# A wait half-way in each chunk's gathers, for ScalarE's copies of the chunk in the other buffer

## The chip, the cores and the metric

The kernel runs on one core of a Trainium2 chip. The metric is the device time of one execution in microseconds. "Profiled execution" means the one that the hardware profiler recorded; "span" is the time from its first to its last recorded instruction.

## The reference, cut to what matters

Two graph networks follow each other over the same 6250 nodes and 200000 edges, sorted by destination. The change touches the second, a transformer over the edges with three layers:

```
src, dst = edge_index[0], edge_index[1]
edge_attr = _mlp(_ln(edge_embed, eng, enb), eW1, eb1, eW2, eb2)
for l in range(L):                                    # L = 3, H = 8 heads, D = 64
    h = _ln(x, n1g[l], n1b[l])
    xi, xj = (h[dst], h[src])
    q = (xi @ Wq[l] + bq[l]).reshape(-1, H, HD)
    kn = (xj @ Wkn[l] + bkn[l]).reshape(-1, H, HD)
    ke = (edge_attr @ Wke[l] + bke[l]).reshape(-1, H, HD)
    vn = (xj @ Wvn[l] + bvn[l]).reshape(-1, H, HD)
    ve = (edge_attr @ Wve[l] + bve[l]).reshape(-1, H, HD)
    alpha = (q * (kn + ke)).sum(-1) / scale
    ...                                               # softmax over the edges of one destination
    msg = ((vn + ve) * alpha[..., None]).reshape(-1, D)
    agg = jax.ops.segment_sum(msg, dst, num_segments=n)
    ...                                               # gate, output product, MLP on the nodes
```

## The kernel before

Edges lie in the order of their destination, 1568 on each of 128 partitions (`T`), and are handled in `NCH` = 28 chunks of `C` = 56 edges a partition. Each layer (`Fori(0, L)`) first makes a table `tabkv` in HBM, one row of 128 floats per node, key and value projection side by side. Then comes the edge loop, `Fori(0, NCH // 2)` with two chunks a turn, `u` = 0 and 1 being the buffer; on ScalarE the last two chunks stand behind the loop. After it, `fix_and_fetch` joins the partitions' ends, and the node part follows. Before all this there is a first part (the first network and the edge MLP), which has gathers of its own from another table.

In the edge loop the engines do this for chunk c, counted over the layers as n:

- GpSimd (line 561 on): waits for the indices `srcI` of the buffer and for `done1`, which VectorE raises at the end of a chunk; it starts at 2 and GpSimd waits for n + 1, so chunk n - 2, the last user of the buffer, must be done. Then `gathers` sends 56 indirect DMAs (line 505), each of which fetches one row of `tabkv` for each of the 128 partitions into `G1[:, u, t, :]`. The semaphore is `got1[u][t // 8]`: eight gathers make one of the seven (`PT`) blocks.
- TensorE (lines 700 to 717): for each step s = 0 to 6 it waits for block s and for free PSUM, and makes keys and values of 8 edges a partition: it copies G1 by the identity (line 712) and adds the edge features' product (line 715). Three pairs of PSUM banks go round, so TensorE may be up to three steps ahead of ScalarE's copies (`v_moved`); the last matmul of a step raises `kv_ready`. With its last step it raises `seen1`, which lets SyncE load new indices.
- VectorE: spreads the queries by eight scans (line 1298), then multiplies the keys of each step by the queries (line 1305, waits for `kv_ready`, raises `k_used`), sums the products (line 1308), scans for the maxima, multiplies the values by the weights (line 1321, reads the value half of G1) and scans them in nine rows (line 1328). Then it raises `done1`.
- ScalarE: after each `k_used` it copies the step's values from PSUM back into the value half of G1 (line 909) and raises `v_moved`. It starts at 3, and seven copies a chunk are made, so 7 n + 3 means that all values of the chunks before n are copied. Then it lays out the next chunk's queries (line 901), makes the exponentials (lines 913 to 915), and stores the chunk's rows (lines 918, 920).
- SyncE loads indices, queries (line 467) and edge features (line 469) for the chunks ahead.

`hold` is a wait followed by one increment of a bookkeeping semaphore that nobody waits for in this loop.

Of the kernel before, what the change touches and what calls it, by code (L numbers as in the profile page):

```python
# [13 lines left out]
C = 56  # L14
NCH = 28
# [12 lines left out]
PT = C // 8  # L28
# [27 lines left out]
def build(nc, A, out):  # L56
# [5 lines left out]
    def dram(name, shape, dt=f32):  # L62
        return nc.dram_tensor(name, shape, dt, kind="Internal").ap()

    tab0 = dram("tab0", (NT * P, W0))
    tabkv = dram("tabkv", (NP, 2 * D))
# [18 lines left out]
    with ctx:  # L85
# [3 lines left out]
        def sem(name):  # L89
            return ctx.enter_context(nc.semaphore(name))  # L90
# [52 lines left out]
        waits_sp, waits_pool, waits_pe = sem("waits_sp"), sem("waits_pool"), sem("waits_pe")  # L143
# [30 lines left out]
        got1 = [[sem(f"got1_{u}_{k}") for k in range(PT)] for u in range(2)]  # L174
# [4 lines left out]
        v_moved = sem("v_moved")  # L179
# [101 lines left out]
        G1 = sb("G1", [P, 2, C, 2 * D])  # L281
# [29 lines left out]
        def hold(eng, passed, s, value):  # L311

            eng.wait_ge(s, value)
            eng.sem_inc(passed, 1)
# [176 lines left out]
        def _(pool):  # L491
# [8 lines left out]
                                      [[1, w], [0, C]], base=0, channel_multiplier=0, **exact)  # L500
            last.then_inc(pool_c, 1)

            def gathers(u, G, tab, got):
                for t in range(C):
                    nc.gpsimd.indirect_dma_start(out=G[:, u, t, :], out_offset=None, in_=tab[:, :],  # L505
                                                 in_offset=IND(ap=srcI[:, u, t:t + 1], axis=0)).then_inc(got(t), 16)


            pool.wait_ge(n0_tab, 16 * NG)
            pool.wait_ge(idx0[0], 16)  # L510
            gathers(0, G0, tab0, lambda t: got0[0])

            pool.wait_ge(p_rp, 16)
# [9 lines left out]
            pool.wait_ge(p_dve, 6)  # L523
            pool.wait_ge(idx0[1], 16)
            gathers(1, G0, tab0, lambda t: got0[1])
            with pool.Fori(1, NCH // 2) as i:
                for u in range(2):
                    pool.wait_ge(idx0[u], 16 * i + 16)
                    hold(pool, waits_pool, done0, 2 * i + u + 1)
                    gathers(u, G0, tab0, lambda t: got0[u])  # L530

            def fix_and_fetch(st, R, o, outs, rows):

                for out_, stored in outs:
                    hold(pool, waits_pool, out_, stored)
                nc.gpsimd.indirect_dma_start(out=rfix[:, 0:R], out_offset=None, in_=st[:, :],
                                             in_offset=IND(ap=fixI[:, 0:1], axis=0)).then_inc(f_got, 16)
                hold(pool, waits_pool, f_dve, o * 5 + 5)
                nc.gpsimd.indirect_dma_start(out=st[:, :], out_offset=IND(ap=fixI[:, 0:1], axis=0),
                                             in_=wfix[:, 0:R], in_offset=None).then_inc(f_put, 16)  # L540
                hold(pool, waits_pool, f_put, o * 16 + 16)
                for j in range(NT):
                    nc.gpsimd.indirect_dma_start(out=rows[:, j, :], out_offset=None, in_=st[:, :],
                                                 in_offset=IND(ap=endI[:, j:j + 1], axis=0)).then_inc(rows_got[j // 8], 16)
# [4 lines left out]
            with pool.Fori(0, L) as l:  # L549

                for j in range(NT):
                    if j % 8 == 0:
                        hold(pool, waits_pool, a_dve, l * A_DVE + 2 * NB + j // 8 + 1)
                    nc.gpsimd.indirect_dma_start(out=qexp[:, :], out_offset=IND(ap=startI[:, j:j + 1], axis=0),
                                                 in_=q_all[:, j, :], in_offset=None).then_inc(q_put, 16)
                hold(pool, waits_pool, q_dram, l * 16 + 16)
                nc.gpsimd.indirect_dma_start(out=qb[:, :], out_offset=None, in_=tabq[:, :],
                                             in_offset=IND(ap=firstI[:, 0:1], axis=0)).then_inc(q_first, 16)
                for k in range(2):
                    hold(pool, waits_pool, a_out[k], (l + 1) * (16 * ((NB + 1 - k) // 2)))  # L560
                hold(pool, waits_pool, h_out, (l + 1) * 32)
                with pool.Fori(0, NCH // 2) as i:
                    for u in range(2):
                        c = 2 * i + u
                        pool.wait_ge(idx1[u], l * (NCH // 2 * 16) + i * 16 + 16)
                        hold(pool, waits_pool, done1, l * NCH + c + 1)
                        gathers(u, G1, tabkv, lambda t: got1[u][t // 8])
                fix_and_fetch(st1, R1, l + 1, [(st1_out, (l + 1) * (16 * NCH) + 16)], rows1)


# [869 lines left out]
```

## Time and profile before

| what | us |
|---|---|
| median of 3 runs | 12879.86 |
| lowest and highest run | 12839.82, 12920.56 |
| profiled execution, its time | 12850.77 |
| its span | 12849.0 |
| GpSimd busy | 7420.7 (58%) |
| VectorE busy | 5378.1 (42%) |
| TensorE matmuls busy | 5153.0 (40%) |
| ScalarE busy | 2820.9 (22%) |

In a row of the timeline the first number is the start in us from the span's start, the second the time it took (of a merged row: the busy time of its xcount instructions), and the brackets hold how long the engine was idle before it and what ended this wait. "issue" there means that the engine waited for nothing the profile shows, and "remote" another core or an unknown queue (this kernel has one core). In the page's group lines, busy time and mean of one stand first behind the bar, then the idle time just before these instructions. TensorE's matmuls are pipelined and their ends are modelled.

### The profile page before, as it was taken

Reading aid. Unit: us, or ns where it says so; the run is one execution under the profiler, and the core shown is the slowest. Engines: PE = TensorE matmul, PEld = TensorE weight load, DVE = VectorE, ACT = ScalarE, POOL = GpSimd, SP = SyncE. Lnnn points to the kernel's source line nnn. Section 1 sums busy time; section 2 is a strip of 40 time slices with the busy share of each in tenths; the row PEclk is TensorE's granted clock in tenths of the full one; section 3 lists DMA queues with packets and bytes.
Section 4 is the critical chain, followed back from the end, with each engine's and each line's share of the span. In section 5 each row is a group of like instructions: output and inputs, shape, how many; then the busy total and the mean of one; then the engine's idle time right before and its main releaser. Section 6 shows DMA issues by size and latency. Waiting matters only on the chain.

```text
span 12849.0 us, 55197 instructions
## 1 busy us (share of the span) xinstructions
PE 5153.0 (40%) x13727; PEld 2796.8 (22%) x13727; DVE 5378.1 (42%) x8026; ACT 2820.9 (22%) x2709; POOL 7420.7 (58%) x6688
## 2 busy tenths in 40 slices
PE   9455554444433333333343333333324233333334
PEld 6322222222211121122211111212112121121122
DVE  3355555544432433444332344344342333433444
ACT  0022222222211211222121122122122112212222
POOL 2488888888745555556525555555544455555552
PEclk9977777777766666666666666666667666666667
DMA  1233333333332322333213223323222222322331
GB/s 33 49 121 120 121 118 111 121 123 111 114 111 77 106 98 97 100 103 119 92 38 104 94 97 106 98 97 110 95 89 73 90 96 94 115 92 95 108 97 46
DMA packets 402907, 1246.37 MB, mean 97 GB/s; under 512 B 194869, under 2 KB 251766, under 8 KB 357926
## 3 DMA queue, kind: packets, MB, share of 16 engines
q0 software_dynamic: 213664, 428.57, 12.7%
q1 hardware_dynamic: 169030, 468.05, 10.3%
q10 hardware_dynamic: 20160, 349.23, 6.9%
q14 instruction: 43, 0.35, 0.0%
q8 instruction: 10, 0.16, 0.0%
HBM read 807.54 MB, written 437.84 MB: 97 GB/s over the span
## 4 chain that ended last, share of the span: by engine, by line
another core or an unknown queue 25%; DVE 22%; issue 19%; POOL 17%; PE 10%; DVEq 3%; ACT 2%; DMA 1%; SPq 0%; ACTq 0%; POOLq 0%
POOL G L505 16%; DVE SX L1328 5%; DVE QQ L1298 5%; DVE SX L1321 4%; PE PS L590 3%; PE PS L712 2%; DVE al L1308 2%; DVE PX L1305 2%; PE PS L715 2%; DVEq L1329 1%; DVEq L1299 1%; DVE SX L1314 1%; PE PS L736 1%; ACT QQ L901 1%
## 5 line engine op out<-in xcount | busy, mean ns | idle before, releaser
L505 POOL DMA_INDIRECT G<-tabkv,srcI x4704 | 4438.4, 944 | 3568.3 <-DVEq L1329 2127.9
L712 PE MATMUL PS<-G,ident 128*128 128x512 f32 x2352 | 1617.4, 826 | 5128.3 <-ACT G L909 3497.1
L505 POOL DMA_INDIRECT G<-tab,srcI x1568 | 2579.8, 1645 | 731.0 <-issue 501.6
L1305 DVE TENSOR_TENSOR PX<-PS,QQ 128x512 f32<-128x512 f32 x588 | 610.2, 1060 | 4647.5 <-remote 3557.6
L712 PEld LDWEIGHTS PS<-G,ident 128*128 128x128 f32 x2352 | 558.8, 252 | 5767.2 <-ACT G L909 3624.3
L715 PE MATMUL PS<-Wkvp,EA 128*128 128x256 f32 x4704 | 1329.9, 422 | 386.0 <-issue 384.9
L909 ACT ACTIVATE G<-PS 128x512 f32<-128x512 f32 x588 | 351.0, 597 | 5133.1 <-issue 3332.1
L644 PE MATMUL PS<-hid,W2p 128*128 128x512 f32 x1568 | 774.4, 640 | 1419.5 <-ACT hid L827 960.4
L715 PEld LDWEIGHTS PS<-Wkvp,EA 128*128 128x128 f32 x4704 | 1050.9, 223 | 930.3 <-issue 803.1
L918 ACT ACTIVATE S<-SX 128x4480 f32<-128x4480 f32 x84 | 688.2, 8193 | 1279.9 <-DVEq L1329 1264.6
L1328 DVE TENSOR_TENSOR_SCAN SX<-PS,SX 128x456 f32<-128x456 f32 x756 | 763.2, 1082 | 12.2
L1298 DVE TENSOR_TENSOR_SCAN QQ<-PS,QQ 128x456 f32<-128x456 f32 x672 | 679.5, 1083 | 209.4 <-issue 145.8
L637 PE MATMUL PS<-xT,W1p 128*128 128x512 f32 x1568 | 715.4, 599 | 76.0 <-ACT xT L806 56.8
L644 PEld LDWEIGHTS PS<-hid,W2p 128*128 128x128 f32 x1568 | 307.3, 206 | 1768.0 <-ACT hid L827 1031.7
L1094 DVE TENSOR_TENSOR al<-G,ewC 128x56 f32<-128x56 f32 x28 | 6.9, 247 | 1415.2 <-DMA G<-tab,srcI 1415.2
L901 ACT ACTIVATE QQ<-QQ 128x3584 f32<-128x3584 f32 x84 | 539.3, 6421 | 264.6 <-DMA QQ<-qexp 264.6
L1321 DVE TENSOR_TENSOR SX<-G,PS 128x3584 f32<-128x3584 f32 x84 | 526.6, 6269 | 87.8 <-ACT PS L914 80.5
L827 ACT ACTIVATE hid<-PS,b1c 128x512 f32<-128x512 f32 x784 | 488.5, 684 | 264.5 <-PE PS L637 254.9
L1124 DVE TENSOR_TENSOR_SCAN S<-ee,S,G 128x56 f32<-128x56 f32 x1792 | 412.8, 317 | 2.1
L1118 DVE TENSOR_TENSOR_SCAN S<-maskC,S,G 128x56 f32<-128x56 f32 x1792 | 411.3, 316 | 0.0
L637 PEld LDWEIGHTS PS<-xT,W1p 128*128 128x128 f32 x1568 | 295.4, 191 | 458.1 <-issue 387.0
L590 PE MATMUL PS<-S 128*49 128x128 bf16 x1568 | 372.2, 416 | 3.4 <-DVE S L1007 3.4
(287 smaller groups left out, 4450.0 us busy)
## 6 DMA issues: line engine op xcount, KB each, us to landing
st<-S ACTq DMA_DIRECT2D x84, 2240.0 KB
QQ<-qexp SPq DMA_DIRECT2D x84, 1792.0 KB
EA<-eaT SPq DMA_DIRECT2D x84, 1792.0 KB
st<-S ACTq DMA_DIRECT2D x28, 3668.0 KB
G<-tabkv,srcI POOLq DMA_INDIRECT x4704
xe<-in_edge_attr SPq DMA_DIRECT2D x28, 1792.0 KB
qexp<-zeros SPq DMA_DIRECT2D x28, 1792.0 KB
eaT<-eaC ACTq DMA_DIRECT2D x28, 1792.0 KB
```

Source lines behind the costliest of these rows:

```text
L505: nc.gpsimd.indirect_dma_start(out=G[:, u, t, :], out_offset=None, in_=tab[:, :], in_offset=IND(ap=srcI[:, u, t:t + 1], axis=0)).then_inc( ...
L590: last = mm(PS[0:NT, 7, 0:P], oh[u][:, t, 0:NT], oh[u][:, t, NT:OHW], start=False, stop=False, skip_group_check=True)
L637: last = mm(PS[:, 1 + 2 * r + kh, :], W1p[:, r, kh, :], xT8[:, :], start=True, stop=True)
L644: last = mm(PS[:, 5, :], W2p[:, kh, r, :], hid8[:, r, kh, :], start=(r == 0 and kh == 0), stop=(r == 1 and kh == 1))
L712: mm(PS[:, b + k, :], ident[:, :], G1[:, u, 8 * s + 4 * k:8 * s + 4 * k + 4, :], start=True, stop=False, skip_group_check=True)
L715: last = mm(PS[:, b + j // 2, 2 * P * (j % 2):2 * P * (j % 2) + 2 * P], EA[:, u, 4 * s + j, :], Wkvp[:, :], start=False, stop=True, skip_g ...
L901: f(Qf[:, :, 1:CX], Q1.rearrange("p c d -> p d c"), ACT.Copy).then_inc(q_flat, 1)
L918: f(S1[:, :, :], SX[:, :, 1:CX].rearrange("p r c -> p c r"), ACT.Copy).then_inc(s_rows, 1)
L1298: scan(rows, gate8f, rows, 0.0, ALU.mult, ALU.add)
L1305: tt(PR[:, 8 * s:8 * s + 8, :], kv_of(b)[:, :, 0:D], Qf[:, :, 1 + 8 * s:9 + 8 * s].rearrange("p d t -> p t d"), ALU.mult).then_inc(k_used, 1)
L1321: tt(SX[:, 2 * H:R1, 1:CX].rearrange("p (j h) x -> p j h x", h=H), G1[:, u, :, D:2 * D].rearrange("p t (h d) -> p d h t", h=H), score8[:, ...
L1328: scan(rows, gate8f, rows, 0.0, ALU.mult, ALU.add)
```

## The change

`gathers` gets a parameter for which of the 56 gathers it sends, all by default. In the edge loop GpSimd sends the first 28, waits until `v_moved` is at 7 n + 3, and sends the other 28.

```
-            def gathers(u, G, tab, got):
-                for t in range(C):
+            def gathers(u, G, tab, got, steps=range(C)):
+                for t in steps:
                     nc.gpsimd.indirect_dma_start(out=G[:, u, t, :], out_offset=None, in_=tab[:, :],
                                                  in_offset=IND(ap=srcI[:, u, t:t + 1], axis=0)).then_inc(got(t), 16)
...
                         pool.wait_ge(idx1[u], l * (NCH // 2 * 16) + i * 16 + 16)
                         hold(pool, waits_pool, done1, l * NCH + c + 1)
-                        gathers(u, G1, tabkv, lambda t: got1[u][t // 8])
+                        gathers(u, G1, tabkv, lambda t: got1[u][t // 8], range(C // 2))
+                        hold(pool, waits_pool, v_moved, (l * NCH + c) * PT + 3)
+                        gathers(u, G1, tabkv, lambda t: got1[u][t // 8], range(C // 2, C))
```

## Rows read from the trace of the kernel before

**Rows 1.** The page: span, then two groups; busy, mean | idle before, its releaser.
```profile
span 12849.0 us, 55197 instructions
L505 POOL DMA_INDIRECT G<-tabkv,srcI x4704 | 4438.4, 944 | 3568.3 <-DVEq L1329 2127.9
L1305 DVE TENSOR_TENSOR PX<-PS,QQ 128x512 f32<-128x512 f32 x588 | 610.2, 1060 | 4647.5 <-remote 3557.6
```

**Rows 2.** The view of line 1305: what ended its idle time (us, times).
```profile
  remote: 3557.6, 174
```

**Rows 3.** The timeline of VectorE over one chunk's steps.
```profile
8104.84 3.00 DVE L1305 TENSOR_TENSOR PX<-PS,QQ 128x512 f32<-128x512 f32 x3
8112.71 1.08 DVE L1305 TENSOR_TENSOR PX<-PS,QQ 128x512 f32<-128x512 f32 x1 [4.88 <-issue]
8129.98 1.05 DVE L1305 TENSOR_TENSOR PX<-PS,QQ 128x512 f32<-128x512 f32 x1 [16.20 <-remote]
8162.18 1.06 DVE L1305 TENSOR_TENSOR PX<-PS,QQ 128x512 f32<-128x512 f32 x1 [31.15 <-remote]
8173.43 1.06 DVE L1305 TENSOR_TENSOR PX<-PS,QQ 128x512 f32<-128x512 f32 x1 [10.19 <-remote]
...
8189.88 9.09 DVE L1328 TENSOR_TENSOR_SCAN SX<-PS,SX 128x456 f32<-128x456 f32 x9
...
8208.89 2.02 DVE L1305 TENSOR_TENSOR PX<-PS,QQ 128x512 f32<-128x512 f32 x2
```

**Rows 4.** The timeline of TensorE in the same chunk, its steps 3, 4 and 6.
```profile
8106.57 3.78 PE L712 MATMUL PS<-G,ident 128*128 128x512 f32 x4 [23.20 <-ACT G L909]
...
8112.51 1.88 PE L712 MATMUL PS<-G,ident 128*128 128x512 f32 x4
...
8119.40 1.88 PE L712 MATMUL PS<-G,ident 128*128 128x512 f32 x4
```

**Rows 5.** The timeline of GpSimd: first and last of these 56 gathers, the next chunk's first.
```profile
8095.30 0.94 POOL L505 DMA_INDIRECT G<-tabkv,srcI  x1 [13.82 <-DVEq L1329]
...
8163.96 0.94 POOL L505 DMA_INDIRECT G<-tabkv,srcI  x1 [0.30 <-issue]
8199.80 0.94 POOL L505 DMA_INDIRECT G<-tabkv,srcI  x1 [34.90 <-DVEq L1329]
```

**Rows 6.** The timeline where two chunks' gathers follow without a gap: GpSimd, then VectorE.
```profile
4877.43 0.94 POOL L505 DMA_INDIRECT G<-tabkv,srcI  x1 [20.85 <-DVEq L1329]
...
5015.98 0.94 POOL L505 DMA_INDIRECT G<-tabkv,srcI  x1 [0.30 <-issue]
...
4983.94 1.05 DVE L1305 TENSOR_TENSOR PX<-PS,QQ 128x512 f32<-128x512 f32 x1 [29.87 <-remote]
5017.54 1.06 DVE L1305 TENSOR_TENSOR PX<-PS,QQ 128x512 f32<-128x512 f32 x1 [32.55 <-remote]
5032.96 3.01 DVE L1305 TENSOR_TENSOR PX<-PS,QQ 128x512 f32<-128x512 f32 x3 [14.36 <-remote]
```

**Rows 7.** The timeline at a layer's start: first gathers of chunks 0 and 1; VectorE.
```profile
3813.45 0.96 POOL L505 DMA_INDIRECT G<-tabkv,srcI  x1 [10.22 <-DMA srcI<-in_src]
...
3883.36 0.94 POOL L505 DMA_INDIRECT G<-tabkv,srcI  x1 [0.30 <-issue]
...
3911.23 1.06 DVE L1305 TENSOR_TENSOR PX<-PS,QQ 128x512 f32<-128x512 f32 x1 [31.84 <-remote]
...
3969.33 2.03 DVE L1305 TENSOR_TENSOR PX<-PS,QQ 128x512 f32<-128x512 f32 x2 [22.75 <-remote]
```

**Rows 8.** Stretches: a layer's first gather of chunk 1 to its last product; length, then busy.
```profile
3883.40:6522.10 2638.70, 898.58 (x2289) 519.63 (x2287) 1073.60 (x975) 544.81 (x327) 1426.71 (x1512) 0.65 0.30 98
6910.40:9553.90 2643.50, 904.46 (x2282) 520.97 (x2281) 1073.29 (x975) 544.87 (x327) 1426.56 (x1512) 0.64 0.30 97
9941.40:12569.40 2628.00, 898.04 (x2285) 519.75 (x2284) 1073.71 (x975) 544.89 (x327) 1426.54 (x1512) 0.64 0.30 98
```

**Rows 9.** The timeline of ScalarE: the last copy of values of the chunk in rows 3.
```profile
8174.52 0.60 ACT L909 ACTIVATE G<-PS 128x512 f32<-128x512 f32 x1 [10.65 <-DVE PX L1305]
```

## Prediction

> **What bounds the kernel now.** I read the page first. The span is 12849.0 us, and the largest groups belong to the layer loops: 4704 gathers on GpSimd, and 588 products of line 1305 on VectorE, before which VectorE sat idle for 4647.5 us, 55 us in each of the 84 chunks [rows 1]. So VectorE is not the bound by its work, and GpSimd is not either, since it too waits for VectorE (`DVEq L1329`) for 2127.9 us [rows 1]. Something keeps both waiting. The view of line 1305 says what ended VectorE's waits: for 3557.6 us "remote", which means that no instruction in the trace explains it [rows 2].
>
> So I followed one chunk in the timeline. VectorE takes steps 0 to 2 together at 8104.84, because TensorE was three ahead, and step 3 at 8112.71. Step 4 it starts at 8129.98, step 5 at 8162.18, step 6 at 8173.43 [rows 3]. The only semaphore it waits for is `kv_ready`, which the last matmul of the step raises. But TensorE's matmuls of steps 3 to 6 begin at 8106.57, the first step taking 5.9 us and each other 3.44 ((8119.40 - 8112.51) / 2), so by the trace step 5 ends at 8119.4 and step 6 at 8122.8 [rows 4]. The signals of steps 5 and 6 therefore reach VectorE 40 to 50 us after the modelled ends of the matmuls. The reader is to see when they come: one per 32 us while GpSimd sends gathers, and then the rest at once.
>
> When is "then"? The gathers of this stretch begin at 8095.30, and the last is issued at 8163.96, so they follow each other by 68.66 / 55 = 1.25 us [rows 5]. The last step starts 78.1 us after the first gather. Elsewhere two chunks' gathers run without a gap, from 4877.43 to 5015.98, 112 of them at the same pace (138.55 / 111 = 1.25). There VectorE gets a step at 4983.94 and one at 5017.54, 33.6 us apart, and then three in 3.01 us at 5032.96, 155.5 us after the first gather [rows 6]. At the start of a layer it is the same: two chunks in a row from 3813.45, a step at 3911.23, and the last two together at 3969.33, 155.9 us after the first [rows 7]. So 56 gathers hold the signals back for 78.1 us and 112 for 155.5 to 155.9 us: 1.39 us a gather, more than the 1.25 us at which they are issued. My reading: something serves 1.39 us for each gather, and while it is behind, a step of TensorE gets through only every 32 to 34 us; when it has caught up, all finished steps get through. I call that moment F. The mechanism itself I can't see in the trace; the rule I read off three places, of two lengths of burst.
>
> The chain of a chunk is then: gathers of chunk n hold back the steps of chunk n-1, VectorE ends chunk n-1 25.5 us after its last step (8173.43 to the end of the nine scans, 8189.88 + 9.09) [rows 3], that raises `done1`, and only then may the gathers of chunk n+1 start. From the first gather of chunk 1 to the last product, the three layer loops take 2638.7, 2643.5 and 2628.0 us [rows 8], 7910.2 in sum; per chunk about 97.
>
> **The change part by part.** It removes nothing and adds one wait per chunk on GpSimd, behind the 28th gather, for the copies of all values of the chunk before (`v_moved`), with one increment of a bookkeeping semaphore. The instruction itself costs well under a microsecond, which I take from how fast GpSimd goes on after such a wait: VectorE's scans end at 8198.97 and the next gather starts at 8199.80 [rows 3, 5]. I take 0.8 us. Queued behind it are 28 gathers of 1.25 us, 35 us of issue, and behind these the gathers of the next chunk; who waits for them is TensorE in steps 3 to 6 of chunk n.
>
> What it does to time follows from F. (a) The first 28 gathers are served after 28 x 1.39 = 38.9 us instead of 77.8, if nothing was pending. (b) At F the remaining steps reach VectorE: three products in 3.0 us [rows 6], ScalarE's last copy starts 1.1 us after the last product starts and takes 0.6 [rows 3, 9], and GpSimd goes on 0.8 us later. So the second half starts at F + 1.95 + 1.1 + 0.6 + 0.8 = F + 4.4. I call this moment R. (c) VectorE goes on from its last product as before and takes the first product of the next chunk 35.5 us later (8173.43 to 8208.89) [rows 3], at R + 33. (d) GpSimd has issued the second half at R + 35. The next chunk's first half needs `done1` of chunk n-1, raised at R - 2.5 + 25.5 = R + 23, so it follows without a gap. GpSimd's waits for `DVEq L1329` go, and those 56 gathers, second half and next first half, are one burst served until R + 56 x 1.39 = R + 77.8. (e) In this burst TensorE must bring the next chunk's seven steps. Steps 0 to 2 it does at once after R, when their blocks have landed (24 gathers of the first half) and nothing is held back yet: in the chunk shown, step 3 still came through 17 us after the burst began [rows 3]. They are ready at R + 33. Step 3 begins at R + 36 and gets through after some 33.5 us, at R + 70. Steps 4 and 5 have run and wait for F. Step 6 needs the copy of step 3, at R + 71.5, and up to 5.9 us on TensorE (the slow first step, 8106.57 to 8112.51) [rows 4], so it ends about at F. (f) At F = R + 77.8 three products, the copy, and the next R is F + 4.4.
>
> The period is then 77.8 + 4.4 = 82.2 us when step 6 is done by F, and about 84 when it misses F by 2 us; I take 83, for 97 before. The wait costs GpSimd 83 - 70 = 13 us a chunk, and this is no loss, since it waited longer for `done1` before.
>
> **The sum**, for one layer loop, from the first gather of chunk 1. To the first R: the burst is then 56 + 28 = 84 gathers from 69.9 us before it [rows 7], so F is at 116.8 - 69.9 = 46.9, and R at 51. Then 26 periods of 83 = 2158. Then from the last R to the last product: products 0 to 2 at 33 to 35, and four steps at TensorE's own pace, because only 28 gathers are in flight, served at 38.9: 5.9 + 3 x 3.44 = 16.2, so 52 in all. Together 2261, for 2638.7, 2643.5 and 2628.0 before. Three layers: 6783 for 7910.2, a gain of 1127. The first part of the kernel doesn't run this code: `gathers` is only given a parameter there, with the old default. The profiled execution took 12850.77 us, 1.8 us over its span, and the median of the runs is 12879.86, 0.2% above it. 12850.77 - 1127 = 11724.
>
> **Bounds of what the trace doesn't show.** It has no break inside a chunk's gathers. How fast the held-back signals come after 28 gathers I bound by nothing faster than the issue itself (35 us) and nothing slower than the share of the long bursts (38.9 us); I take the latter, since three bursts of two lengths fit it. For how soon after R steps are held back again, the bounds are 17 us and more (the step that got through in rows 3) and, at the worst, at once; I take the 17, which is enough to have steps 0 to 2 through. The worse end is the first rival. Nothing bounds the loss at zero: if the signals don't come in the break, GpSimd stands still and its gathers come later.
>
> **The rivals.** *The break is too short.* The signals of steps 1 and 2 are not out before the service is behind again. Then step 1 comes at about R + 67, and steps 2 and 3 only at F. Step 5 needs the copy of step 2 and step 6 that of step 3, so TensorE runs both after F: 1.8 + 5.9 + 3.4 = F + 11.1, R is 2.5 us behind that, and the period is about 91. 51 + 26 x 91 + 52 = 2469 a layer, 7407 for the three, 503 less than before: about 12350. For it: in the chunk of rows 3 only step 3 comes through in the burst before the 32 us rhythm begins, and the break is only 4 us. Against it: at 5032.96 three steps come in 3 us, so what is pending goes at once.
>
> *The signals don't depend on the gathers* (slower). They come late by a clock of their own, 57 to 78 us after the chunk began, whatever GpSimd does. Then the wait ends 60 to 80 us after the first gather, on average 73; 35 us of gathers follow, and the period is 73 + 35 = 108 for 97: 81 x 11 = 890 more, 13740. The point from which it decides: the change loses when the wait ends later than 97 - 35 = 62 us after the chunk's first gather. Against it: 155.5 us for 112 gathers and 78.1 for 56 are the same 1.39 each; a clock of its own would not scale. By the Trainium skill, "SBUF — State Buffer", section "Who interferes with whom", this would be the case: a DMA never contends with a compute engine, and PE waits on no one. The trace does not agree as far as it goes: the steps' signals stop and go with the gathers, by 40 to 50 us; what the two share it does not tell.
>
> *Nothing changes.* The copies are all done when the wait is reached, 35 us after the chunk's first gather. In the chunk shown the last copy starts at 8174.52, 79 us after it [rows 9], so this can be so in few chunks: 12850.
>
> *Nothing is held back at all*, because no burst is long: GpSimd then issues without pause, 70 us a chunk, 11724 - 26 x 3 x 13 = about 10700. Against it: the service, not the issue, would then be behind again, as in the bursts of 112.
>
> **How the numbers follow.** The forecast (period 82 to 86, 11650 to 11960) gets 0.6, the too short break 0.22, the signals on their own clock 0.1, no change 0.04, nothing held back 0.04. The predicted time is that of the first, 11724. The range must reach to the second, 12350, and a period 1.3 us longer (26 x 3 x 1.3 = 100): 12450. At the other end, a service that has caught up a microsecond sooner, as the scatter of the bursts allows, gives a period of about 81, 2 us under the 83, 26 x 3 x 2 = 156: 11570, and I begin at 11550. Left out is 0.1 + 0.04 + 0.04. Faster by over 1%: 0.6 + 0.22 + 0.04 = 0.86; within 1%: 0.04; slower by over 1%: 0.1. About 1% is what a measurement of this kernel can tell from no change, its three runs lying 0.6% apart.
>
> **What would show it.** In the profile after: GpSimd's waits for `DVEq L1329` nearly gone in the layer loops, and in their place one of some 13 us per chunk before the 29th gather, ended by ScalarE's copies (L909), about 1000 us in all. VectorE with three products in 3 us just ahead of that gather's start. VectorE's idle time before line 1305 down from 55 to about 41 us a chunk. Gathers still 944 ns, 1.25 us apart. The forecast is wrong if the 29th gather starts much later than 45 us after a layer's burst of 28, or if VectorE still gets single steps 32 us apart behind the break.

## The result, and the profile after

| what | us |
|---|---|
| changed kernel, median of 4 runs | 11651.4 (11649.46 to 11656.92) |
| kernel before, beside it, median of 4 | 12859.84 (12741.78 to 12920.56) |
| ratio | 0.9058, 95% interval 0.9014 to 0.9102 |
| forecast | 11724, range 11550 to 12450 |

The change makes the kernel 9.4% faster. One sentence belongs to this number from the start, though nothing in the profile before hinted at it: in two of the later jobs the kernel before itself took 10547 and 10560 us, and in the one of them in which the changed kernel ran too, the change is worth nothing (run `after_b` below).

The page of the changed kernel first, the same groups as in [rows 1]; all lines behind 566 have moved by 2 (1305 is 1307 now, 909 is 911, 1328 is 1330; in the kernels of the experiments the lines move by some others, and the names of the tiles stay):

```profile
span 11655.1 us, 55365 instructions
L505 POOL DMA_INDIRECT G<-tabkv,srcI x4704 | 4438.9, 944 | 2460.5 <-issue 1408.0
L1307 DVE TENSOR_TENSOR PX<-PS,QQ 128x512 f32<-128x512 f32 x588 | 602.5, 1058 | 3430.5 <-remote 3216.5
```

A gather still takes 944 ns. GpSimd's idle time before gathers fell from 3568.3 to 2460.5 us, VectorE's before its products from 4647.5 to 3430.5, 55.3 to 40.8 us a chunk. VectorE's end of a chunk no longer stands among what GpSimd waits for. The view of GpSimd's waits (us in total, times, longest) has ScalarE's copies in its place:

```profile
POOL G L505 <- issue: 1909.5, 6187, 2.2
POOL G L505 <- ACT G L911: 1021.9, 81, 17.3
```

The timeline of GpSimd around two waits, and of VectorE between them:

```profile
7128.09 0.94 POOL L505 DMA_INDIRECT G<-tabkv,srcI  x1 [0.30 <-issue]
7141.09 0.94 POOL L505 DMA_INDIRECT G<-tabkv,srcI  x1 [12.06 <-ACT G L911]
...
7209.74 0.94 POOL L505 DMA_INDIRECT G<-tabkv,srcI  x1 [0.30 <-issue]
7223.17 0.94 POOL L505 DMA_INDIRECT G<-tabkv,srcI  x1 [12.48 <-ACT G L911]
...
7155.21 9.09 DVE L1330 TENSOR_TENSOR_SCAN SX<-PS,SX 128x456 f32<-128x456 f32 x9
...
7174.99 2.99 DVE L1307 TENSOR_TENSOR PX<-PS,QQ 128x512 f32<-128x512 f32 x3
7185.31 1.07 DVE L1307 TENSOR_TENSOR PX<-PS,QQ 128x512 f32<-128x512 f32 x1 [7.33 <-remote]
7216.11 1.05 DVE L1307 TENSOR_TENSOR PX<-PS,QQ 128x512 f32<-128x512 f32 x1 [29.73 <-remote]
7219.70 2.06 DVE L1307 TENSOR_TENSOR PX<-PS,QQ 128x512 f32<-128x512 f32 x2 [2.53 <-remote]
```

The second half starts at 7141.09 (this is the R of the prediction), and 56 gathers run without a gap until 7209.74. The last two steps come together at 7219.70, 78.6 us after R. The next R is 3.5 us later, at 7223.17: 82.1 us for this chunk. The layer loops, first gather of chunk 1 to last product as in [rows 8]:

```profile
3891.00:6128.00 2237.00, 799.82 (x2291) 480.38 (x2289) 1079.14 (x976) 545.94 (x327) 1426.80 (x1512) 0.67 0.34 115
6515.20:8750.00 2234.80, 793.11 (x2288) 476.37 (x2289) 1078.88 (x975) 546.24 (x328) 1426.77 (x1512) 0.68 0.34 115
9139.90:11376.70 2236.80, 795.93 (x2286) 478.74 (x2284) 1078.21 (x975) 545.93 (x327) 1426.82 (x1512) 0.67 0.35 115
```

The second stretch ends 1.3 us too early, for that layer's last product starts at 8751.25. So it is about 6710 us for 7910, 1200 less, and the profiled execution took 1193.9 less than before (11656.92 for 12850.77). All of the gain is in the layer loops. The busy time of VectorE, ScalarE and GpSimd has hardly changed there; that of TensorE's matmuls, as the trace models them, went from 2701 to 2389 us, but TensorE waits for most of a loop in both kernels. It is waiting that went.

One thing more stands in this trace, and it was in that of the kernel before too: not only the signals are late. Towards the end of the step that TensorE makes last before its long wait, its own matmuls come one by one. Its timeline in the same chunk:

```profile
7194.39 0.38 PE L717 MATMUL PS<-Wkvp,EA 128*128 128x256 f32 x1 [2.29 <-issue]
7197.19 0.40 PE L717 MATMUL PS<-Wkvp,EA 128*128 128x256 f32 x1 [2.42 <-issue]
```

They are 2.80 us apart, with one weight load between them, so 1.40 us an instruction. Inside a step, two matmuls of this line start 2.8 us apart in 82 places of this trace and in 34 of the kernel before's, where 2.1 us, in 54, is more frequent; in the later runs in which nothing is held back (`after_b`, `e_sw`) they are never more than 0.4 us apart.

### The profile page after: what moved, and what is told of

Read it like the earlier page. It is cut to its first block, busy times and chain, and to the rows that moved or that the text cites. A ratio compares the mean times of both kernels' runs of the same rounds, so it can differ in the third digit from the quotient of the medians.

```text
span 11655.1 us, 55365 instructions
## 1 busy us (share of the span) xinstructions
PE 4839.1 (42%) x13727; PEld 2670.5 (23%) x13727; DVE 5393.2 (46%) x8026; ACT 2825.5 (24%) x2709; POOL 7427.5 (64%) x6688
## 3 DMA queue, kind: packets, MB, share of 16 engines
q1 hardware_dynamic: 169030, 468.05, 11.1%
## 4 chain that ended last, share of the span: by engine, by line
another core or an unknown queue 30%; DVE 27%; issue 18%; PE 10%; DVEq 5%; POOL 5%; ACT 3%; DMA 2%; SPq 0%; ACTq 0%; POOLq 0%
DVE SX L1330 6%; DVE QQ L1300 5%; DVE SX L1323 4%; POOL G L505 3%; PE PS L592 3%; DVE PX L1307 2%; PE PS L646 2%; DVE al L1310 2%; PE PS L639 2%; DVE S L1126 2%; DVE S L1120 2%; DVEq L1309 1%; ACT QQ L903 1%; DVEq L1331 1%
## 5 line engine op out<-in xcount | busy, mean ns | idle before, releaser
L505 POOL DMA_INDIRECT G<-tabkv,srcI x4704 | 4438.9, 944 | 2460.5 <-issue 1408.0
L714 PE MATMUL PS<-G,ident 128*128 128x512 f32 x2352 | 1435.0, 742 | 4252.3 <-ACT G L911 3390.1
L1307 DVE TENSOR_TENSOR PX<-PS,QQ 128x512 f32<-128x512 f32 x588 | 602.5, 1058 | 3430.5 <-remote 3216.5
L714 PEld LDWEIGHTS PS<-G,ident 128*128 128x128 f32 x2352 | 519.7, 230 | 4839.8 <-ACT G L911 3559.6
L717 PE MATMUL PS<-Wkvp,EA 128*128 128x256 f32 x4704 | 1207.5, 395 | 377.4 <-issue 377.3
L717 PEld LDWEIGHTS PS<-Wkvp,EA 128*128 128x128 f32 x4704 | 963.0, 205 | 783.6 <-issue 680.6
L554 POOL DMA_INDIRECT qexp<-PX,startI x147 | 140.9, 958 | 369.9 <-DVEq L1288 326.0
```

Of the source, the lines that this page charges most:

```text
L714: mm(PS[:, b + k, :], ident[:, :], G1[:, u, 8 * s + 4 * k:8 * s + 4 * k + 4, :], start=True, stop=False, skip_group_check=True)
L717: last = mm(PS[:, b + j // 2, 2 * P * (j % 2):2 * P * (j % 2) + 2 * P], EA[:, u, 4 * s + j, :], Wkvp[:, :], start=False, stop=True, skip_g ...
L1307: tt(PR[:, 8 * s:8 * s + 8, :], kv_of(b)[:, :, 0:D], Qf[:, :, 1 + 8 * s:9 + 8 * s].rearrange("p d t -> p t d"), ALU.mult).then_inc(k_used, 1)
```

## The experiments

Theory 1 is that of the prediction: gathers in flight hold back TensorE's step signals, with 1.39 us of service for each; when it has caught up, at F, all pending steps come. Jobs are independent, and each has its own runs of the kernel before; ratios are only taken inside a job.

**The first job: where the wait stands, what it waits for, and how much TensorE does.** The kernel before took 12851.24 us in it (median of 7).

`e_kv` waits for TensorE's last signal instead of ScalarE's last copy:

```
-                        hold(pool, waits_pool, v_moved, (l * NCH + c) * PT + 3)
+                        hold(pool, waits_pool, kv_ready, (l * NCH + c) * PT + 1)
```
(`kv_ready` starts at 1 in it, and VectorE's wait for it is one higher.)

> The changed kernel, but GpSimd's wait behind the 28th gather is for the last step's signal from TensorE (kv_ready) instead of ScalarE's last copy (v_moved). Theory 1 (the gathers in flight hold back TensorE's step signals; when their service has caught up, at a moment F, all pending ones go, and GpSimd may go on): the changed kernel goes on 3.4 us after F (two products 1.95 us apart with 1.1 + 0.6 for the copy and 0.8 for GpSimd); here it goes on 0.8 us after F, so the period falls from 82.0 to about 79.6 us, 78 periods x 2.4 = 190 us, 11460 us. Rival (the copies themselves must be out of the way before the gathers go on, because the gathers hold up ScalarE or VectorE as well): no gain or a loss, 11650 us or more.

Measured: 11518.24 us (11506.52 to 11525.44), ratio 0.8979, interval 0.8915 to 0.9044. GpSimd goes on 1.0 us after the pending steps come, in the timeline of VectorE and GpSimd:

```profile
7401.87 3.01 DVE L1308 TENSOR_TENSOR PX<-PS,QQ 128x512 f32<-128x512 f32 x3 [8.11 <-PE PS L717]
...
7402.86 0.94 POOL L505 DMA_INDIRECT G<-tabkv,srcI  x1 [10.30 <-PE PS L717]
```

The mean period is 80.4 us, for 82.0 of the changed kernel. Theory 1 gave 79.6 and 11460 us; the median period is 79.9, but some take up to 83.5. So the gain is some 133 us for the 190 that were expected. The rival, that the gathers must wait for the copies themselves, falls. This is the fastest version that computes the whole result, about 130 us (1.1%) under the changed kernel, each measured in its own job; the periods' difference, 78 x 1.6 = 125, says the same.

`e_at0` has the wait ahead of the chunk's first gather, `e_at44` behind the 44th:

```
-                        gathers(u, G1, tabkv, lambda t: got1[u][t // 8], range(C // 2))
+                        gathers(u, G1, tabkv, lambda t: got1[u][t // 8], range(0))
                         hold(pool, waits_pool, v_moved, (l * NCH + c) * PT + 3)
-                        gathers(u, G1, tabkv, lambda t: got1[u][t // 8], range(C // 2, C))
+                        gathers(u, G1, tabkv, lambda t: got1[u][t // 8], range(C))
```

> The changed kernel with the same wait, but ahead of the first gather instead of behind the 28th. Theory 1 (all that counts is one pause per 56 gathers in which TensorE's signals get out, wherever it is): burst of 56 gathers, F 77.8 to 78.8 us after it began, GpSimd on 3.4 to 4.4 us later, period 82 to 83 us, 11650 to 11750 us. Rival (the gain comes from the place: half a chunk's gathers are sent ahead while the chunk before is at work, and a full chunk's can't be late): a chunk's gathers start only when the chunk before is copied, so its last blocks land 70 us later and the steps 3 to 6 follow them one by one; period 90 us or more, 12270 us or more, and slower than the kernel before (12860) if the signals came by a clock of their own.

Measured: 12093.15 us, ratio 0.9429 (0.9362 to 0.9497), mean period 87.6 us. Both missed. Between the two: the service is as theory 1 has it, but a step is late behind it. The gathers of this stretch begin at 7735.6:

```profile
7804.43 0.95 POOL L505 DMA_INDIRECT G<-tabkv,srcI  x1 [0.31 <-issue]
7812.98 3.02 DVE L1307 TENSOR_TENSOR PX<-PS,QQ 128x512 f32<-128x512 f32 x3 [18.59 <-remote]
7814.72 3.78 PE L714 MATMUL PS<-G,ident 128*128 128x512 f32 x4 [9.10 <-ACT G L911]
7820.92 1.06 DVE L1307 TENSOR_TENSOR PX<-PS,QQ 128x512 f32<-128x512 f32 x1 [4.92 <-PE PS L717]
7823.42 0.95 POOL L505 DMA_INDIRECT G<-tabkv,srcI  x1 [18.04 <-ACT G L911]
```

At 7812.98, 77.4 us after the first gather, three steps come at once, 3, 4 and 5. Step 6 couldn't be made before, because TensorE needs the copy of step 3 for its PSUM. It begins at 7814.72, and the next gather is only 10.4 us behind the moment F, not 3.4. In the changed kernel step 3 comes early, since its gathers are in the first half or just behind the wait, and step 6 is ready at F. So the place does count, through this one dependency; I had left it out of what I expected here, though the prediction has it, in its first rival.

> The changed kernel with the same wait behind the 44th gather. Theory 1: after the wait only 12 gathers are left, issued in 15 us, and the next chunk's first must wait for VectorE's end of the chunk, 23 us after the wait. So a burst of 44 starts at R + 24, is served until R + 24 + 61 = R + 85, and the next wait ends 3.4 us later: period about 88.5 us, 6.5 more than the changed kernel's 82.0, 78 x 6.5 = 507 more: 12160 us, with GpSimd again waiting some 8 us a chunk for VectorE's last scan. Rival (a later pause lets the gathers get further ahead and does no harm, since VectorE's steps come at their own pace): 11650 us or less.

Measured: 12090.61 us, ratio 0.9433 (0.9365 to 0.95), mean period 86.4 to 87.0 us in the three layers for 88.5. The rival falls, and theory 1 has the time to 0.6%, a little high; single periods scatter from 79 to 97 us, which it doesn't explain. GpSimd waits twice a chunk, in its timeline for the copies and then for VectorE's last scan:

```profile
7754.92 0.94 POOL L505 DMA_INDIRECT G<-tabkv,srcI  x1 [0.30 <-issue]
7765.15 0.94 POOL L505 DMA_INDIRECT G<-tabkv,srcI  x1 [9.28 <-ACT G L911]
...
7778.88 0.94 POOL L505 DMA_INDIRECT G<-tabkv,srcI  x1 [0.30 <-issue]
7789.15 0.94 POOL L505 DMA_INDIRECT G<-tabkv,srcI  x1 [9.33 <-DVEq L1331]
```

It also adds a third length of burst to the rule. The first of 44 gathers, and VectorE's last product before the wait ends:

```profile
7701.27 0.94 POOL L505 DMA_INDIRECT G<-tabkv,srcI  x1 [9.33 <-DVEq L1331]
7762.67 1.07 DVE L1307 TENSOR_TENSOR PX<-PS,QQ 128x512 f32<-128x512 f32 x1 [0.45 <-remote]
```

That is 61.4 us for 44, 1.40 a gather.

`e_noea` is the kernel before with less work for TensorE:

```
                             for k in range(2):
-                                mm(PS[:, b + k, :], ident[:, :], G1[...], start=True, stop=False, skip_group_check=True)
-                            for j in range(4):
-                                last = mm(PS[...], EA[:, u, 4 * s + j, :], Wkvp[:, :], start=False, stop=True, ...)
+                                last = mm(PS[:, b + k, :], ident[:, :], G1[...], start=True, stop=True, skip_group_check=True)
                             last.then_inc(kv_ready, 1)
```

> The kernel before, with TensorE's edge-feature product (line 715, 8 of the 12 matmul records of a step, with as many weight loads) left out, so the keys and values lack the edge features; everything else, gathers and waits too, as before. Theory 1a (while the gathers are behind, TensorE gets through instruction by instruction, about one per gather, 24 per step now: 24 x 1.39 = 33 us a step): with 8 instructions a step the held back steps come 11 us apart, VectorE's last step at about 45 us after the chunk's first gather instead of 57 to 78, and the kernel is faster: period about 78 us, near 11300 us. Rival 1b (it is held back by the step, whatever is in it): steps stay 32 us apart, and the time stays within 2% of 12860 us.

Measured: 11294.35 us in two runs, ratio 0.8807 (0.8725 to 0.889). Time and period are those of theory 1a, and rival 1b falls. A line of its page:

```profile
L505 POOL DMA_INDIRECT G<-tabkv,srcI x4704 | 4918.3, 1046 | 1633.9 <-issue 1603.2
```

Its timeline of VectorE, three steps in a burst, and of TensorE, the last two of them:

```profile
7308.56 1.05 DVE L1302 TENSOR_TENSOR PX<-PS,QQ 128x512 f32<-128x512 f32 x1 [8.75 <-remote]
7319.75 1.05 DVE L1302 TENSOR_TENSOR PX<-PS,QQ 128x512 f32<-128x512 f32 x1 [10.13 <-remote]
7330.95 1.06 DVE L1302 TENSOR_TENSOR PX<-PS,QQ 128x512 f32<-128x512 f32 x1 [10.14 <-remote]
...
7311.57 3.78 PE L712 MATMUL PS<-G,ident 128*128 128x512 f32 x4 [6.40 <-DMA G<-tabkv,srcI]
7322.99 3.78 PE L712 MATMUL PS<-G,ident 128*128 128x512 f32 x4 [7.65 <-DMA G<-tabkv,srcI]
```

With 8 instructions a step instead of 24 (weight loads counted) no step is held back for 32 to 34 us any more. They come 11.2 us apart, which is 8 times 1.40 us. But this number doesn't show that the instruction is the unit, for a step also needs eight gathers, and 8 x 1.39 is 11.1 as well: by the rows TensorE starts each step when its gathers have landed, and the product follows 8 us behind that start. For the unit there are the total time, which 1b had unchanged, and TensorE's matmuls 2.80 us apart in the changed kernel, shown above. And GpSimd now waits for nobody: (4918.3 + 1633.9) / 84 = 78.0 us a chunk, 56 x 1.39, where its own issue would take 70. The gathers themselves are slowed, to a mean of 1046 ns: over half of the 4704 still take 0.95 us or less, and of the 213 that take 1.45 us or more, 150 fall on the 3.8 us of a step's matmuls. So in this run TensorE's work slows the gathers too. That the service would keep to 1.39 us wherever the wait is, so that about 78 us a chunk is a floor (the changed kernel is at 82, `e_kv` at 80.4), fits all runs of these jobs but is not shown.

**The second job: what about the gathers does it?** Here the kernel before took 12546.85 us (one run). Both kernels below ran once, and both fetch other values than the edges need.

```
-                        gathers(u, G1, tabkv, lambda t: got1[u][t // 8])
+                        for t in range(C):
+                            r = t % 49 * P
+                            nc.gpsimd.dma_start(G1[:, u, t, :], tabkv[r:r + P, :]).then_inc(got1[u][t // 8], 16)
```

This is `e_sw`; in `e_hw` the same 56 DMAs are issued by SyncE behind the load of EA.

> The kernel before, with each indirect gather of the layer loops replaced by a plain DMA of the same size from the same GpSimd queue (rows of the table in order, not by index), so the values fetched are not those of the edges. Theory 2a (any DMA that GpSimd makes in software holds the signals back): steps still some 30 us apart while they are sent, time within a few per cent of 12860 us. Rival 2c (only the indirect form does it): steps follow at 3.4 us, some 10000 us.

> The kernel before, with each indirect gather of the layer loops replaced by a plain DMA of the same size (128 rows of 512 bytes out of the same table, rows in order, not by index) issued from SyncE's queue behind the edge features' load; GpSimd sends none in the edge loop. The values fetched are not those of the edges. Theory 2 (it is the software-made gathers of GpSimd, not the bytes moved, that hold back TensorE's signals): nothing is held back, VectorE's steps follow TensorE's at 3.4 us, and the chunk is bound by VectorE and its neighbours, some 60 us: 84 x 37 less, 9700 us. Rival 2b (it is the traffic into G1, 3.7 MB a chunk, that holds TensorE back): steps still come 30 us apart, and the time stays near 12860 us.

Measured: 9222.03 us for `e_sw`, 9221.24 us for `e_hw`, both less than the 10000 and 9700 of their forecasts, with a period of 54 us for some 60. Nothing is held back in either, in the timeline of VectorE in `e_sw`:

```profile
6306.92 1.08 DVE L1307 TENSOR_TENSOR PX<-PS,QQ 128x512 f32<-128x512 f32 x1 [4.62 <-PE PS L717]
6310.36 1.08 DVE L1307 TENSOR_TENSOR PX<-PS,QQ 128x512 f32<-128x512 f32 x1 [2.37 <-PE PS L717]
6313.81 1.08 DVE L1307 TENSOR_TENSOR PX<-PS,QQ 128x512 f32<-128x512 f32 x1 [2.37 <-PE PS L717]
6317.25 1.07 DVE L1307 TENSOR_TENSOR PX<-PS,QQ 128x512 f32<-128x512 f32 x1 [2.37 <-PE PS L717]
```

Two single runs could owe this to the job instead. They don't: the first part of the kernel, whose gathers were left as they are, shows in which sort of job a trace was taken. The view of the DMAs gives a time to landing where the trace has the increments of the semaphores, 16 for each DMA. In `e_sw` it has them for the plain DMAs and not for the first part's gathers, in `after_b`, where nothing is held back, for both:

```profile
G<-tabkv POOLq DMA_DIRECT2D x4704, 64.0 KB, 3.7
G<-tab,srcI POOLq DMA_INDIRECT x1568
```

```profile
G<-tabkv,srcI POOLq DMA_INDIRECT x4704, 2.5
G<-tab,srcI POOLq DMA_INDIRECT x1568, 2.6
```

Counted in the traces, the first part's gathers have 11984 of their 25088 increments in `e_sw` and 11429 in the kernel before, where steps are held back, and 25086 in `after_b`. So `e_sw` and `e_hw` (11885) ran where gathers do hold the steps back, and all 75264 increments of their plain DMAs are there. Nor is it the pace: GpSimd issues a plain DMA every 0.53 us, a gather every 1.25.

So the bytes don't do it, nor the queue of GpSimd as such: theories 2a and 2b fall. What is left is the indirect form or the scattered rows that it reads.

**The next two jobs: another state of affairs.** `e_ord` keeps the indirect form and takes the indices from a fixed table `ordI`, rows in order, which GpSimd makes once ahead of the loop (not shown); `e_half2` leaves out every second gather.

```
-                        gathers(u, G1, tabkv, lambda t: got1[u][t // 8])
+                        for t in range(C):
+                            nc.gpsimd.indirect_dma_start(out=G1[:, u, t, :], out_offset=None, in_=tabkv[:, :],
+                                                         in_offset=IND(ap=ordI[:, t:t + 1], axis=0)).then_inc(got1[u][t // 8], 16)
```

> The kernel before, with the same 56 indirect gathers a chunk, but their indices from a fixed table (rows in order, 128 t + p, t from 0 to 48 and again from 0) instead of srcI, so the values are not those of the edges. It stands between the kernel before and the one with plain DMAs of rows in order (9222 us). Theory 3 (the indirect form is what holds TensorE's signals back, wherever the rows lie): steps 32 us apart, 78 us to the last one, within 2% of the kernel before. Rival 3b (the random addresses do it): steps 3.4 us apart, GpSimd issuing 70 us a chunk is the bound, about 84 x 27 less, 10600 us.

> The kernel before, with every second gather of the edge loop left out (28 per chunk; the other rows of G1 keep what lay there, zeros at first), and TensorE waiting for half the count. Theory 1: the 28 gathers are served 38.9 us after the first, the steps pending come together at about 39 to 40 us, VectorE ends the chunk 25.5 us later, and the next chunk's gathers start: period about 66 to 68 us against 97, some 84 x 30 = 2500 less, 10350 us. Rival (the late steps have a clock of their own and come 57 to 78 us after the chunk's start): period unchanged, 12860 us.

Measured: `e_ord` 10548.85 us beside the kernel before at 10547.22, ratio 1.0002 (0.9991 to 1.0013); `e_half2` 9167.03 us (one run). The kernel before was 18% faster than in the first job, and neither test could decide: where nothing is held back, there is nothing to take away. In the following job the two were tried again, as `e_ord3` and `e_half3`, with the changed kernel beside them.

> The changed kernel again, beside the two others. On a chip where before takes near 12850 us: 11650 us. On a chip where before takes 10547 us, and where GpSimd sends 70 us a chunk without a pause: theory 1: steps there come some 10 us apart beside the gathers, so at the 28th gather, 35 us after the chunk's first, the last copy of the chunk before is 5 to 15 us away or done; each microsecond of wait is lost, since GpSimd is the bound, 82 x 0 to 10, so 10550 to 11300 us: the same or slower than before. Rival (the change gains wherever it runs): 9550 us.

The kernel before took 10560.38 us (15 runs, 10557.91 to 10564.97). `e_ord3` took 10560.87, `e_half3` 9156.48 (one run; 9167 was expected for such a job), and the changed kernel 10560.64: ratio 1.0 (0.9988 to 1.0011), no difference at all. It is the same program as the one at 11651 us, and this job ran on the same chip as the first job of the experiments. The page of `after_b`:

```profile
L505 POOL DMA_INDIRECT G<-tabkv,srcI x4704 | 4448.4, 946 | 1453.3 <-issue 1433.2
L1307 DVE TENSOR_TENSOR PX<-PS,QQ 128x512 f32<-128x512 f32 x588 | 607.9, 1056 | 2422.8 <-PE PS L717 2422.8
```

Its timeline, VectorE's last product of a chunk and ScalarE's copy behind it:

```profile
6989.17 1.06 DVE L1307 TENSOR_TENSOR PX<-PS,QQ 128x512 f32<-128x512 f32 x1 [8.86 <-PE PS L717]
6990.26 0.60 ACT L911 ACTIVATE G<-PS 128x512 f32<-128x512 f32 x1 [9.32 <-DVE PX L1307]
```

"remote" is gone: each wait of VectorE ends with TensorE's matmul, as it should. The steps are some 10 us apart here because TensorE waits for the eight gathers of each, 8 x 1.25. GpSimd waits for nothing but its own issue, (4448.4 + 1453.3) / 84 = 70.3 us a chunk, and is the bound. The last copy starts at 6990.26, 8 us after the next chunk's first gather at 6982.2. When GpSimd reaches the wait, 35 us after that gather, it is long past. I had allowed a wait of up to 10 us; there was none.

**The last job** was `e_ord` once more:

> The kernel before with indices from a fixed table (rows in order) for the same 56 indirect gathers; the values are not those of the edges. A third time, because in the two jobs before the kernel before itself took 10547 and 10560 us and nothing was held back there. If before takes near 12850 us in this job: theory 3 (the indirect form holds TensorE's signals back): steps 32 us apart, within 2% of before. Rival 3b (the random addresses do it): no step is held back, GpSimd's issue is the bound, 10550 us. If before takes 10550 us: the same as before, and the question stays open.

This time the kernel before took 12600.32 us, and `e_ord4` 12631.82, ratio 1.0032 (1.0001 to 1.0063). Its steps are held back as before, in VectorE's timeline beside 112 gathers from 7789.3:

```profile
7891.25 1.06 DVE L1312 TENSOR_TENSOR PX<-PS,QQ 128x512 f32<-128x512 f32 x1 [29.06 <-remote]
7924.85 1.06 DVE L1312 TENSOR_TENSOR PX<-PS,QQ 128x512 f32<-128x512 f32 x1 [32.54 <-remote]
7944.46 3.01 DVE L1312 TENSOR_TENSOR PX<-PS,QQ 128x512 f32<-128x512 f32 x3 [18.55 <-remote]
```

33.6 us apart, and three together 155.2 us after the first gather, the numbers of [rows 6]. With theory 3 it is the indirect form, wherever the rows lie; 3b falls.

What stays open: why the same kernels are held back in most jobs (before at 12547 to 12880 us) and not in two (10547 and 10560), one of these on the chip of the first. No kernel here controls it. One rival stands untested: that recording has a part in it. All times here are of runs whose span and clock were recorded, and where steps are held back the traces have lost most increments of the gathers' semaphores: the kernel before has 13830 of the 75264 of its edge loops, the changed kernel 11817, `after_b` 75002. No run shows whether the loss is an effect, a cause or a bystander. Lost increments alone cost no time in the first part: the first gather of the edge loops comes at 3813.5 us in the kernel before and at 3813.0 in `after_b`.

`e_half` only ran in the jobs where nothing is held back. But each layer of the changed kernel ends with 28 gathers alone, the first of them, and VectorE behind them:

```profile
6076.42 0.94 POOL L505 DMA_INDIRECT G<-tabkv,srcI  x1 [12.53 <-ACT G L911]
...
6117.06 1.08 DVE L1307 TENSOR_TENSOR PX<-PS,QQ 128x512 f32<-128x512 f32 x1 [4.49 <-PE PS L717]
6120.51 1.07 DVE L1307 TENSOR_TENSOR PX<-PS,QQ 128x512 f32<-128x512 f32 x1 [2.37 <-PE PS L717]
```

Step 3 comes 40.6 us after the first gather, just as TensorE has made it, and the others follow at 3.44 us. So 28 gathers hold nothing back for longer than that, which fits 38.9 us.

## Why the prediction was right, point by point

**What bounds the kernel** (held back signals, one moment F at 1.39 us a gather): right. F was at 78.6 us in the changed kernel, 61.4 for 44 gathers in `e_at44`, 77.4 in `e_at0`, 155.2 in `e_ord4`, and `e_noea` has the 1.39 us as a rate of the gathers themselves. What I did not see was that the held back unit seems to be the instruction, at 1.4 us, and that TensorE's own matmuls are slowed and not only their signals.

**(b), from F to R**: 4.4 us forecast, 3.5 measured. Two products come at F, not three, because step 4 comes 3.6 us ahead of F (7216.11). Mis-sized by one product, in each of the 78 periods.

**(e), step 3**: wrong. It was to need 33.5 us, but came at 7185.31, 8.6 us after TensorE began it (at 7176.7 by its timeline, 1.7 us behind the first product). It is step 4 that takes the long wait, 30.8 us behind. TensorE had been idle for 25 us before it, and the first step after such a pause came 7.6 to 9.6 us after its start in all 78 periods; in the kernel before, step 3 came at once too, behind an idle time of 23.2 us [rows 3, 4]. It did not change the sum, because the last steps waited for F in any case.

**(f), the period**: 83 us forecast, 82.0 measured. The 0.8 us that I had added for chunks in which step 6 misses F was never needed. That the 82.2 without it is met so closely is partly luck: F came 0.8 us later than I had it (78.6 for 77.8), and R 0.9 us sooner behind it, by (b). The period makes up the difference: 78 periods x 0.95 = 74 us, and the layer loops took about 6710 us for the forecast 6783. The first R of a layer came at 52 us (3943.0 - 3891.0) for 51, the last product 51 to 52 us after the last R for 52.

**The first rival** (the break is too short) did not happen here: in each of the 78 periods the last two products come together at F. `e_at0` shows its mechanism, a step 6 that can only be made after F, at a period of 87.6 us.

**The second rival** (signals with a clock of their own) falls with `e_sw`, where a GpSimd without indirect gathers leaves the signals alone, and with `e_noea`. The rule of the Trainium skill that goes with it ("SBUF — State Buffer", section "Who interferes with whom": a DMA never contends with a compute engine, PE waits on no one) is not borne out, taken at its word, where steps are held back: matmuls of one step start 2.80 us apart, and in `e_noea` a gather takes 1046 ns instead of 944. In the jobs at 10550 us it is, for each of VectorE's waits ends with TensorE's matmul. That section is about the ports of SBUF, and no run here shows that a port is what the two share.

**The third** (nothing changes) I gave 0.04, for a reason that the trace denied, copies already done at the wait. In the jobs at 10550 us it is precisely what happens. A trace shows one state of the machine, and the forecast held for that state. That the changed kernel was measured in the state of the trace was luck.

**The fourth** (nothing held back at all, 10700 us, 0.04) did not come about by the change: GpSimd still waited 1021.9 us for the copies. Its price is nearly that of the jobs at 10550 us, where GpSimd does issue without pause at 70 us a chunk, but there the kernel before takes as long.

**What would show it**: GpSimd's waits for ScalarE about 1000 us in all, measured 1021.9; VectorE's idle time 41 us a chunk, measured 40.8; the waits for VectorE's scans gone, and in the edge loops they are.

## What to carry to other kernels

When an engine waits and the trace names no releaser, look for a unit of time that fits several stretches of different length: 78 us for 56 gathers and 155.5 for 112 gave the rule, and the rule gave the time to 0.6%, though what is shared was not known and still is not. Where a queue's work holds back another engine's signals, one pause per round lets them out, and it should end on the earliest signal that shows they are out (`kv_ready`, 1.1% better than `v_moved`, each measured in its own job). And measure such a change in several jobs: this wait is worth 9.4% where the signals are held back and 0.0% where they are not, and it costs nothing there, since it is passed before it is reached.

## What the runs showed of the hardware that I had not expected

- In most of these jobs indirect gathers of 128 rows of 512 bytes and TensorE's instructions hold each other back. Finished steps come out 78 us after the first of 56 gathers, 61 for 44 and 155 for 112, 1.39 us a gather, though a gather is issued every 1.25 us. While gathers are in flight a step of 24 instructions takes 32 to 34 us, and single matmuls are 2.80 us apart, 1.4 us per TensorE instruction. Plain DMAs of the same size from the same queue do not do this: steps 3.44 us apart, 9222 us.
- Rows in order or scattered make no difference: ratio 1.0032 (1.0001 to 1.0063) with held back signals, 1.0002 (0.9991 to 1.0013) and 1.0 (0.9989 to 1.0011) without.
- The same program on the same chip took 12851 us in one job and 10560 in another, with a scatter of 2% in the first and 0.07% in the second. The traces of the slower kind lack most of the gathers' semaphore increments (13830 of 75264 there), those of the other kind have nearly all (75002). A cause was not found.
